# Settling without the high and low split, 64-column w1 products, zeros and biases earlier, experts' inputs five pairs ahead

## The chip, the cores and the metric

One core of one Trainium2 chip. The time is the device time of one execution in microseconds (us), the median of several runs.

## What is computed

Two layers over 8192 tokens (16 sequences of 512) of 256 channels. Layer 0 adds to x, from its layer norm, a small gated network on four heads and a mixture of experts; layer 1 adds an attention and a product with a ternary matrix.

```python
xn = _layernorm(x, axis=-1)
x = x + _L0_attn_ref(xn, ...) + _L0_ffn_ref(xn, ...)
xn = _layernorm(x, axis=-1)
x = x + _L1_attn_ref(xn, ...) + _L1_ffn_ref(xn, ...)

# _L0_ffn_ref, 16 experts, the best two of each token
xe = jnp.einsum('bsd,eod->bseo', u, Wr) + br
routed = jnp.einsum('bse,bseo->bso', g_topk, xe)
shared = (jnp.einsum('bsd,eod->bso', u, Ws) + jnp.sum(bs, axis=0)) / N_s
return u + routed + shared

# _L1_ffn_ref
out = jnp.einsum('bsd,od->bso', input, w_ternary * alpha) + bias
```

The gated network needs only the query part of `_L0_attn_ref` in this kernel: q is normalised, goes through w0 and w2 (`tanh` makes the sigmoid), and the hidden vector goes through w1.

## The kernel before

`two_layers` runs four stages one after the other. Each is a block: all five queues (SP, POOL, ACT, DVE, PE) end it together before the next begins. A unit is U = 2 tiles of 128 tokens; there are NU = 32 units. Every engine runs a fixed, written-out list of steps, so the order on each engine is the order of the code, and semaphores do the rest. An SP or POOL queue that waits holds back all transfers behind the wait.

**1. Sorting stage, `route`.** Steps v from -6 to 34; a step works on units v to v+4 at different places of the pipeline. PE: w0 and w2 products in two halves (L609, 64-row tiles), counts of the chosen experts (L621 to L662), transposes (L633, L654), the query and score product (L644), and `psB`, which takes the shared expert (L677) and w1 (L680). ACT evaluates tanh (L348), squares with a sum (L372), copies and normalised rows (L391). DVE multiplies the hidden vector (L439, L442), scales the queries (L536, L545) and chooses the experts (L454 to L489). POOL takes roots and powers and scatters each normalised row to its two experts' regions in `rows_dram` (L313). w1 is kept as 128 columns per head of which 64 are zero, so that both heads of a pair add into all 128 partitions of one bank. In the last steps SP reads, expert by expert, the end of each region into a register (`value_load`) and writes 128 rows of zeros there (L267, 16 transfers), writes two small tables (L260), and stores the parts of the last units (L250). After its last step DVE makes the low halves of the experts' weights (L593, 16 instructions of 128x512).

**2. Experts, `experts`.** 72 pairs of jobs; a job is 128 rows for one expert. SP loads a pair's rows three pairs ahead (`xs`, XS = 8 slots, L753) and stores the pair's result (L762) after waiting for DVE; PE transposes pair n+1 (L816) and then multiplies pair n with 12 products (L834 to L836: high by high, high by low, low by high); ACT takes the high part of the transposed rows (L782), DVE the low part (L790) and adds the expert's bias (L801). The biases of all experts (128 x 4096 numbers) are loaded by SP behind the first six loads (L757). The registers with table entries are loaded eight at a time.

**3. Settling, `settle`.** Per unit: SP loads the part and x (L894, L896) three units ahead, POOL gathers the two expert results of each of the two tiles with four indirect transfers (L939), PE transposes the part (L1041), DVE adds x, the two weighted results, takes mean and variance, adds the bias of the last product (`x1b`, L1012), makes six small factors (L1016 to L1025); POOL takes the root (L948, L950); ACT normalises (L959); PE transposes (L1052); ACT takes the high part (L965), DVE the low part (L975), PE multiplies both with the ternary matrix (L1059, L1060), DVE adds up `base` (L983). SP stores high part, low part and base (L912, L916, L918). SP also loads the first weights of the last stage here.

**4. Attention, `phase_b`.** 256 heads, one per step, 16 steps per sequence. SP loads the high and low parts of the next sequence in step 12 (L1207, L1208). Before the first product ACT and DVE split the first weights (L1323, L1415).

What sets the order in the experts' loads:

```python
for j in range(3 * U):
    load(j)
sp.dma_start(bias_bc[:], io["br"]...partition_broadcast(P)).then_inc(br_in, 16)
for n in range(PAIRS):
    for t in range(U):
        load((n + 3) * U + t)
    need(sp, y_dve, U, n, U)
    sp.dma_start(out_dram[n], ys[:, n % 4]).then_inc(y_out[n % 4], 16)
```

Of the kernel before, what the change touches and what calls it, by code (L numbers as in the profile page):

```python
# [21 lines left out]
F32 = mybir.dt.float32  # L22
# [5 lines left out]
P = 128  # L28
D = 256
# [55 lines left out]
class Kept:  # L85


    def __init__(self, nc, ctx, tiles, jobs):
# [9 lines left out]
        self.wtern = sb("wtern", [P, KD, D], F32R)  # L98
        self.alpha_bc = sb("alpha_bc", [P, 1])
        self.table = sb("table", [1, 2 * 2 * P], mybir.dt.uint32)  # L100

# [7 lines left out]
def route(nc, io, rows, part, region, jobs, kept, raw, wr_hi, raw_in):  # L109
# [5 lines left out]
    with ExitStack() as ctx:  # L115
# [6 lines left out]
        def bank(name, n=1):  # L122
# [3 lines left out]
        w1 = sb("w1", [P, FH, P])  # L126
# [4 lines left out]
        raw_s = sb("raw_s", [P, KD, NS, D])  # L131
        raw_t = sb("raw_t", [P, KD, D])
# [3 lines left out]
        tern = sb("tern", [P, 2, KD, D])  # L136
# [23 lines left out]
        junk = sb("junk", [P, 2, U, D])  # L160
        z2 = sb("z2", [P, 2, U, D])
# [3 lines left out]
        qn = sb("qn", [P, 2, U, D])  # L165
        qt = sb("qt", [P, 2, FH // 2, U, P])
        th = sb("th", [P, 8, 2, U * P])
        acc = sb("acc", [P, 2, U, D])
# [28 lines left out]
         rt_dve, rt_act, c_pe, tb_dve, tb_in, ends_in) = map(sem, (  # L197
             "const_in", "const_pool", "const_dve", "w1_act", "wr_act", "wr_dve", "tern_dve", "tern_pe", "ln_dve", "ln_pool",
             "ln_act", "t_pe", "t_act", "r_pe", "r_act", "r_dve", "z_pool", "zs_dve", "zq_dve", "q_pe", "q_act",
             "g_pe", "g_act", "g_dve", "b_pe", "b_act", "rt_dve", "rt_act", "c_pe", "tb_dve", "tb_in",  # L200
# [3 lines left out]
        POOL_CONST = 4 + 3 + 1 + 2 + 3 + 4  # L204
# [15 lines left out]
        def _(sp):  # L220
# [25 lines left out]
            for v in steps:  # L246
                u = v - 2
                if 0 <= u < NU:
                    need(sp, b_act, 1, u, 1)
                    sp.dma_start(part[u], acc[:, u % 2]).then_inc(stored[u % 2], 16)  # L250
# [6 lines left out]
                if v == NU:  # L257
                    sp.wait_ge(tb_dve, 13)
                    for k in range(2):
                        sp.dma_start(kept.table[0:1, k * 2 * P:(k + 1) * 2 * P].rearrange("a (p h) -> a p h", p=P),  # L260
                                     jobs_u[:, k]).then_inc(tb_in, 16)
# [10 lines left out]
            sp.wait_ge(tb_in, 32)  # L272
            for r in range(2):
                sp.wait_ge(stored[r], 16 * (NU // 2))

        @block.gpsimd
        def _(g):
# [10 lines left out]
            const(g.memset(w1[:], 0.0))  # L288
# [1421 lines left out]
```

## Time and profile before

| | us |
|---|---|
| median of 3 runs | 3041.45 |
| lowest, highest | 3036.73, 3049.71 |
| the profiled execution: its time | 3047.77 |
| the profiled execution: its span | 3046.0 |
| busy PE, DVE, ACT, POOL | 2774.1, 2111.6, 1841.7, 1995.8 |
| mean granted TensorE clock | 0.952 of full speed |

The profiled execution's own time is 1.8 us more than its span, which goes from its first to its last instruction. Busy times are sums over four stages of very different limits. The queues of the transfers and semaphore instructions are not counted as busy. In a timeline each row gives the start, the duration, engine, line and operation, what it writes and reads, and in brackets how long the engine had been idle before it and what released it. A product of plain float32 numbers has two records on PE, one of the fp32r kind has one.

### The profile page before, as it was taken

Reading aid. Unit: us, or ns where it says so; the run is one execution under the profiler, and the core shown is the slowest. Engines: PE = TensorE matmul, PEld = TensorE weight load, DVE = VectorE, ACT = ScalarE, POOL = GpSimd, SP = SyncE. Lnnn points to the kernel's source line nnn. Section 1 sums busy time; section 2 is a strip of 40 time slices with the busy share of each in tenths; the row PEclk is TensorE's granted clock in tenths of the full one; section 3 lists DMA queues with packets and bytes.
Section 4 is the critical chain, followed back from the end, with each engine's and each line's share of the span. In section 5 each row is a group of like instructions: output and inputs, shape, how many; then the busy total and the mean of one; then the engine's idle time right before and its main releaser. Section 6 shows DMA issues by size and latency. Waiting matters only on the chain.

```text
span 3046.0 us, 46091 instructions
## 1 busy us (share of the span) xinstructions
PE 2774.1 (91%) x13314; PEld 2043.3 (67%) x13314; DVE 2111.6 (69%) x3578; ACT 1841.7 (60%) x2651; POOL 1995.8 (66%) x1246
## 2 busy tenths in 40 slices
PE   6999678555499999999999999999999999999997
PEld 4555377444366777777777777777777777777775
DVE  6878555688766666767676766667666666767663
ACT  4555222122267777767676777777777777777774
POOL 4666500477257777777777777777777777777775
PEclk9999899666699999999999999999999999999998
DMA  4432367798512232222222222232322222231321
GB/s 135 133 124 91 134 206 216 219 266 254 176 42 67 49 74 54 68 69 52 69 54 68 58 64 63 58 76 45 74 53 71 58 62 75 43 79 43 79 48 48
DMA packets 271646, 282.95 MB, mean 93 GB/s; under 512 B 97344, under 2 KB 214336, under 8 KB 271424
## 3 DMA queue, kind: packets, MB, share of 16 engines
q1 hardware_dynamic: 259264, 248.25, 30.8%
q0 software_dynamic: 12288, 33.57, 3.6%
q8 instruction: 44, 0.72, 0.1%
q14 instruction: 50, 0.41, 0.0%
HBM read 131.76 MB, written 82.31 MB: 70 GB/s over the span
## 4 chain that ended last, share of the span: by engine, by line
PE 70%; POOL 1%; DVE 1%; ACT 1%; DMA 0%; issue 0%; SPq 0%; POOLq 0%; ACTq 0%; DVEq 0%
PE psV_b L1581 8%; PE psV_b L1576 8%; PE psV_b L1577 8%; PE psS_b L1564 8%; PE psS_b L1563 7%; PE psN_b L1549 7%; PE psY_b L1504 4%; PE psX_b L1504 4%; PE psY_b L1505 4%; PE psY_b L1506 4%; PE psX_b L1505 4%; PE psX_b L1506 4%; POOL pp_lo_b L1294 1%; PE psN_b L1633 0%; DVE vals_lo_b L1472 0%
## 5 line engine op out<-in xcount | busy, mean ns | idle before, releaser
L1294 POOL TENSOR_TENSOR pp_lo_b<-pf_b,pp_hi_b 128x1024 fp32r<-128x1024 f32 x512 | 1229.7, 2402 | 604.3 <-ACT pp_hi_b L1336 517.9
L1440 DVE TENSOR_REDUCE negmax_b<-psN_b 128x2 fp32r<-128x1024 f32 x512 | 626.9, 1224 | 379.1 <-PE psN_b L1549 371.8
L1331 ACT ACTIVATE pf_b<-psS_b 128x1024 f32<-128x1024 f32 x512 | 526.1, 1028 | 238.4 <-PE psS_b L1564 235.2
L1563 PE MATMUL psS_b<-qA_b,kA_b 128*128 128x512 f32 x1024 | 405.8, 396 | 6.8 <-DVE qB_b L1455 5.0
L1564 PE MATMUL psS_b<-qB_b,kB_b 68*128 68x512 f32 x1024 | 406.6, 397 | 0.0
L1577 PE MATMUL psV_b<-pp_hi_b,vals_lo_b 128*64 128x512 f32 x1024 | 403.6, 394 | 0.0
L1576 PE MATMUL psV_b<-pp_hi_b,vals_hi_b 128*65 128x512 f32 x1024 | 402.0, 393 | 1.7 <-DVE vals_lo_b L1472 0.2
L1355 ACT ACTIVATE kA_b<-psX_b 64x512 fp32r<-64x512 f32 x256 | 152.0, 594 | 289.4 <-PE psX_b L1506 284.6
L1549 PE MATMUL psN_b<-kA_b,qA_b 128*128 128x512 f32 x1024 | 322.6, 396 | 4.7 <-DVE negmax_b L1440 4.2
L1581 PE MATMUL psV_b<-pp_lo_b,vals_hi_b 128*65 128x512 f32 x1024 | 320.2, 394 | 5.1 <-POOL pp_lo_b L1294 5.1
L1336 ACT ACTIVATE pp_hi_b<-pf_b 128x1024 fp32r<-128x1024 f32 x256 | 271.5, 1061 | 8.1
L1429 DVE SCALAR_TENSOR_TENSOR kB_b<-psX_b,kA_b 64x512 fp32r<-64x512 f32 x256 | 176.2, 688 | 140.1 <-ACT kA_b L1355 136.0
L1563 PEld LDWEIGHTS psS_b<-qA_b,kA_b 128*128 128x128 f32 x1024 | 193.6, 189 | 65.9 <-DVE qB_b L1455 7.2
L1450 DVE CAST pp_hi_b<-pf_b 128x1024 fp32r<-128x1024 f32 x256 | 233.0, 910 | 5.3 <-ACT pf_b L1331 5.3
L1549 PEld LDWEIGHTS psN_b<-kA_b,qA_b 128*128 128x128 f32 x1024 | 192.2, 190 | 55.1 <-DVE negmax_b L1440 7.2
L1308 POOL TENSOR_TENSOR otf_b<-outs,inverse_b 128x512 f32<-128x512 f32 x128 | 211.1, 1649 | 20.8 <-DMA inverse_b<-inverse_dram 18.6
L1504 PE MATMUL psX_b<-xT_hi,wqkv_hi_b 128*128 128x512 f32 x512 | 210.8, 412 | 13.9 <-DVE wqkv_lo_b L1415 8.4
L1564 PEld LDWEIGHTS psS_b<-qB_b,kB_b 68*128 68x128 f32 x1024 | 193.6, 189 | 40.5
L1581 PEld LDWEIGHTS psV_b<-pp_lo_b,vals_hi_b 128*65 128x65 f32 x1024 | 137.7, 135 | 105.7 <-POOL pp_lo_b L1294 9.7
L1505 PE MATMUL psX_b<-xT_lo,wqkv_hi_b 128*128 128x512 f32 x512 | 203.7, 398 | 0.0
L1506 PE MATMUL psX_b<-xT_hi,wqkv_lo_b 128*128 128x512 f32 x512 | 203.4, 397 | 0.0
L1429 DVE SCALAR_TENSOR_TENSOR qA_b<-psX_b,qA_b 64x512 fp32r<-64x512 f32 x256 | 176.5, 690 | 38.2 <-ACT qA_b L1355 34.2
(209 smaller groups left out, 5623.6 us busy)
## 6 DMA issues: line engine op xcount, KB each, us to landing
kA_b<-kA_b SPq DMA_DIRECT2D x128, 256.0 KB, 3.2
qB_b<-qA_b SPq DMA_DIRECT2D x128, 256.0 KB, 2.9
inverse_b<-inverse_dram SPq DMA_DIRECT2D x256, 128.0 KB, 3.1
xs_e<-rows_dram SPq DMA_DIRECT2D x144, 128.0 KB, 2.6
results_dram<-ys_e SPq DMA_DIRECT2D x72, 256.0 KB, 2.4
x_a<-x_dram SPq DMA_DIRECT2D x16, 512.0 KB, 4.7
part_dram<-acc_a SPq DMA_DIRECT2D x32, 256.0 KB
acc_s<-part_dram SPq DMA_DIRECT2D x32, 256.0 KB
```

The lines of the kernel that those rows point to most:

```text
L1294: pool.tensor_tensor(pp[1][:, c], pf[:, c], pp[0][:, c].bitcast(F32), ALU.subtract).then_inc(pl_pool, 1)
L1331: a.activation(pf[:, c], psS[:], ACT.Exp).then_inc(exp_act, 1)
L1440: v.tensor_reduce(negmax[:, n.slot(2), 2 * c:2 * c + 2], psN[:], AX.X, ALU.max, negate=True).then_inc(mx_dve, 1)
L1504: pe.matmul(out, lh, rh, start=start, stop=False)
L1505: pe.matmul(out, lh, rl, start=False, stop=False)
L1506: return pe.matmul(out, ll, rh, start=False, stop=stop)
L1549: mm = pe.matmul(psN[:, t], qA[:, s, i * P:(i + 1) * P], kA[:, s], start=True, stop=True)
L1563: pe.matmul(psS[:, t], kA[:, s, keys], qA[:, s], start=True, stop=False)
L1564: mm = pe.matmul(psS[:, t], kB[:, s, keys], qB[:, s], start=False, stop=True)
L1576: pe.matmul(psV[0:DH + 1, g.slot(2)], values(0, h, i), pp[0][:, c, t], start=(i == 0), stop=False)
L1577: pe.matmul(psV[0:DH, g.slot(2)], values(1, h, i), pp[0][:, c, t], start=False, stop=False)
L1581: mm = pe.matmul(psV[0:DH + 1, g.slot(2)], values(0, h, i), pp[1][:, c, t], start=False, stop=(i == TB - 1))
```

## The change

- `route`: w1 is kept as 64 columns per head; the two heads of a pair write partitions 0 to 63 and 64 to 127 of the bank. The bias load is moved from the experts to step 17 of this stage. The 16 zero writes and both tables are issued by SP in step NU-1, ahead of the part of that step, with eight ends loaded into registers at once. DVE makes the low halves of four weight pieces after the tables, of four more before the last hidden product, and of eight at the end. `raw_s`, `raw_t`, `tern` lie in the bias tile, `junk`, `z2`, `qn`, `acc` in the tiles that the settling loads into.
- `experts`: twelve slots and loads five pairs ahead; no bias load and no wait for it; near the end SP issues the first three units' loads of the settling.
- `settle`: the part and x are joined on PE (x by identity, then the part against the identity, both into one bank); no DVE addition of x, no `x1b`, no low part; the ternary product is plain float32 of the unsplit rows; one transposed copy is stored (two stores per unit fewer); the factors of unit u follow the sums of unit u+1 and the end of unit u-1; POOL gathers two units at first and a third after the root.
- `phase_b`: one load of the unsplit rows per sequence (step 11) into two slots of `ot`; ACT makes the high part (step 12), DVE the low part in two pieces (steps 12 and 13); the ternary bias is added by DVE in steps 3 to 6. For the first sequence both parts are made ahead of the first product.

```diff
@@ route
-                if NU - 1 <= v <= NU:
-                    if v == NU - 1:
-                        sp.wait_ge(tb_dve, 1)
-                    for e in range((v - NU + 1) * NE // 2, (v - NU + 2) * NE // 2):
-                        at = sp.value_load(ends_u[0:1, e:e + 1], min_val=0, max_val=NE * region - P)
-                        sp.dma_start(rows[bass.ds(at, P), :], zeros[:]).then_inc(ends_in, 16)
+                if v == 17:
+                    sp.wait_ge(tern_dve, 11)
+                    sp.dma_start(bias_bc[:], io["br"].rearrange("e n -> (e n)").partition_broadcast(P)).then_inc(br_in, 16)
+                if v == NU - 1:
+                    sp.wait_ge(tb_dve, 1)
+                    for h in range(2):
+                        at = nc.values_load_multi_w_load_instructions(
+                            ends_u[0:1, h * 8:(h + 1) * 8], engines=[mybir.EngineType.SP], min_val=0, max_val=NE * region - P,
...
+                        for e in range(8):
+                            sp.dma_start(rows[bass.ds(at[e], P), :], zeros[:]).then_inc(ends_in, 16)
...
                 if s == NU - 1:
                     make_tables()
+                    weights_low(0, 4)
...
+                if s == NU - 1:
+                    weights_low(4, 8)
                 if 0 <= s < NU:
                     hidden_product(s, 1)
...
+            weights_low(8, 16)
...
-                        mm = pe.matmul(psB[:, 0], w1[:, 2 * m + j], th[:, first:first + 3:2, j], start=False, stop=(j == 1))
+                        mm = pe.matmul(psB[j * FD:(j + 1) * FD, 0], w1[:, 2 * m + j], th[:, first:first + 3:2, j], start=False, stop=True,
+                                       skip_group_check=True)
@@ experts
-        XS = 8
+        XS = 12
...
-            for j in range(3 * U):
+            for j in range(5 * U):
                 load(j)
-            sp.dma_start(bias_bc[:], io["br"].rearrange("e n -> (e n)").partition_broadcast(P)).then_inc(br_in, 16)
             for n in range(PAIRS):
                 for t in range(U):
-                    load((n + 3) * U + t)
+                    load((n + 5) * U + t)
                 need(sp, y_dve, U, n, U)
                 sp.dma_start(out_dram[n], ys[:, n % 4]).then_inc(y_out[n % 4], 16)
+                if n >= PAIRS - 5 and n < PAIRS - 2:
+                    ahead.load(sp, n - PAIRS + 5)
@@ settle
-            for u in range(3):
-                gather(u)
+            gather(0)
+            gather(1)
             for u in range(NU):
-                need(g, s_dve, SD, u, 9)
-                need(g, s_dve, SD, u - 2, SD)
+                need(g, s_dve, SD, u, SD)
+                need(g, f_dve, FC, u - 2, FC)
...
-                gather(u + 3)
+                if u < 2:
+                    gather(u + 2)
+                if u >= 1:
+                    gather(u + 3)
...
+            for u in range(NU + 2):
+                if u < NU:
+                    gathered(u)
+                if 0 <= u - 1 < NU:
+                    factors(u - 1)
+                finish(u - 2)
...
                     for t in range(U):
+                        pe.matmul(psA[:, u % 2, t * D:(t + 1) * D], kept.ident[:], x[:, u % 4, t], start=True, stop=False,
+                                  skip_group_check=True)
                         for m in range(KD):
                             at = (t * KD + m) * P
-                            mm = pe.transpose(psA[:, u % 2, at:at + P], acc[:, u % 4, m, t * P:(t + 1) * P], kept.ident[:])
+                            mm = pe.matmul(psA[:, u % 2, at:at + P], acc[:, u % 4, m, t * P:(t + 1) * P], kept.ident[:], start=False,
+                                           stop=True, skip_group_check=True)
...
-                        pe.matmul(out, xrt[0][:, u % 2, t, k], kept.wtern[:, k], start=(k == 0), stop=False)
-                        mm = pe.matmul(out, xrt[1][:, u % 2, t, k], kept.wtern[:, k], start=False, stop=(k == KD - 1))
+                        mm = pe.matmul(out, xrt[:, u % 2, t, k], kept.wtern[:, k], start=(k == 0), stop=(k == KD - 1))
@@ phase_b
-            for c in SPLITS[-4]:
+            split_low(0)
+            for k in range(KD):
+                rows_low(Step(None, 1, 0), xT[1][:], k)
+            for c in SPLITS[-4][1:]:
                 split_low(c)
```

## Rows read from the trace of the kernel before

**Rows 1.** Stages: us, busy PE, PEld, DVE, ACT, POOL, clock, DMA share, GB/s.

```profile
60.00:360.00 300.00, 274.02 (x1276) 162.37 (x1276) 235.94 (x698) 155.32 (x361) 197.41 (x203) 0.99 0.35 116
...
380.00:558.00 178.00, 142.29 (x1118) 133.30 (x1116) 102.17 (x214) 41.33 (x69) 7.74 (x14) 0.96 0.69 209
...
580.00:740.00 160.00, 85.35 (x352) 68.99 (x352) 142.31 (x421) 37.16 (x66) 114.61 (x133) 0.63 0.88 258
...
1000.00:1500.00 500.00, 499.73 (x2365) 370.20 (x2364) 348.00 (x441) 356.48 (x470) 368.76 (x179) 1.00 0.27 64
```

**Rows 2.** Timeline of the sorting stage, the round from one count to the next.

```profile
197.18 0.30 PE L621 MATMUL psC_a<-mask_a,before_a 128*128 128x64 f32 x1 [0.57 <-DVE mask_a L480]
...
198.14 2.00 PE L644 MATMUL psR_a<-wq_a,xt_a 128*128 128x272 f32 x8
...
201.05 0.69 DVE L545 TENSOR_TENSOR qw_a<-psR_a,qw_bc_a 128x512 f32<-128x512 f32 x1 [0.53 <-ACT junk_a L372]
...
204.29 1.88 PE L680 MATMUL psB_a<-th_a,w_a 128*128 128x512 f32 x4
...
207.66 0.58 ACT L348 ACTIVATE th_a<-psG_a 128x512 f32<-128x512 f32 x1
...
216.88 0.30 PE L621 MATMUL psC_a<-mask_a,before_a 128*128 128x64 f32 x1 [0.77 <-DVE mask_a L480]
```

**Rows 3.** Timeline of the sorting stage's end and the first row of the experts.

```profile
338.47 0.17 DVE L500 TENSOR_TENSOR ends_u_a<-psC_a,ebase_a 128x16 uint32<-128x16 f32 x1
...
348.87 9.71 DVE L593 TENSOR_TENSOR wr_raw<-wr_raw,wr_hi 128x512 fp32r<-128x512 f32 x16
...
355.62 0.69 ACT L365 ACTIVATE acc_a<-psB_a,mean_b_a 128x512 f32<-128x512 f32 x1 [3.85 <-PE psB_a L680]
...
357.19 7.97 SPq L267 DMA_DIRECT2D rows_dram<-zeros_a  x8
365.20 0.43 SPq L250 DMA_DIRECT2D part_dram<-acc_a  x1
367.83 0.29 POOL L768 COPY moved_e<-place_f 128x128 f32<-128x128 f32 x1 [21.52 <-POOLq L115]
```

**Rows 4.** Timeline of the experts; the last row is the loads' time from issue to landing.

```profile
381.03 0.76 DVE L801 TENSOR_TENSOR ys_e<-psY_e,bias_bc_e 128x256 f32<-128x256 f32 x2 [4.87 <-DMA bias_bc_e<-br_dram]
...
383.86 0.42 SPq L762 DMA_DIRECT2D results_dram<-ys_e  x1
...
385.37 0.43 SPq L762 DMA_DIRECT2D results_dram<-ys_e  x1
...
387.93 0.51 PE L816 MATMUL psT_e<-ident_r,xs_e 128*128 128x128 f32 x4 [0.39 <-DMA xs_e<-rows_dram]
...
549.43 0.46 PE L816 MATMUL psT_e<-ident_r,xs_e 128*128 128x128 f32 x4
...
551.23 0.46 PE L816 MATMUL psT_e<-ident_r,xs_e 128*128 128x128 f32 x4
...
DMA to landing us min/median/max: 2.0/2.6/7.4
```

**Rows 5.** Timeline of the settling; last, one of DVE's groups (busy us, mean ns).

```profile
558.36 0.36 SPq L894 DMA_DIRECT2D acc_s<-part_dram  x1
...
624.07 0.20 POOL L948 TENSOR_TENSOR vs_s<-mv_s,eps_s 128x4 f32<-128x4 f32 x1 [0.73 <-DVE stats_s L1006]
...
631.41 0.20 POOL L948 TENSOR_TENSOR vs_s<-mv_s,eps_s 128x4 f32<-128x4 f32 x1 [1.06 <-DVE mv_s L1010]
...
L1012 DVE TENSOR_TENSOR x1b_s<-x_s,fbias_bc_s 128x512 f32<-128x512 f32 x22 | 15.0, 680 | 0.0
```

**Rows 6.** Timeline of the attention: its start, and ACT after step 12.

```profile
810.26 0.91 SPq L1204 DMA_DIRECT2D pf_b<-w_qkv_dram  x2
...
815.25 0.76 PE L1504 MATMUL psX_b<-xT_hi,wqkv_hi_b 128*128 128x512 f32 x1 [8.41 <-DVE wqkv_lo_b L1415]
...
1224.88 1.03 ACT L1331 ACTIVATE pf_b<-psS_b 128x1024 f32<-128x1024 f32 x1 [1.20 <-PE psS_b L1564]
```

More of the change, by code:

```diff
@@ L247, in _ @@
                 u = v - 2
+                if v == 17:
[6 more added lines that the diff above has]
+                            ends_u[0:1, h * 8:(h + 1) * 8], engines=[mybir.EngineType.SP], min_val=0, max_val=NE * region - P,
+                            skip_runtime_bounds_check_because="an end is a region's base and a count of at most N rows", bass_reorder=False)[1]
+                        for e in range(8):
+                            sp.dma_start(rows[bass.ds(at[e], P), :], zeros[:]).then_inc(ends_in, 16)
+                    sp.wait_ge(tb_dve, 13)
+                    for k in range(2):
+                        sp.dma_start(kept.table[0:1, k * 2 * P:(k + 1) * 2 * P].rearrange("a (p h) -> a p h", p=P),
+                                     jobs_u[:, k]).then_inc(tb_in, 16)
                 if 0 <= u < NU:
@@ L519, in make_tables, with weights_low @@
                                        op0=ALU.mult, op1=ALU.add).then_inc(tb_dve, 1)
+            def weights_low(first, end):
+                for c in range(first, end):
+                    at = weights_of_experts(c)
+                    v.wait_ge(wr_act, c + 1)
+                    v.tensor_tensor(raw[at].bitcast(F32R), raw[at], wr_hi[at].bitcast(F32), ALU.subtract).then_inc(wr_dve, 1)
             for s in steps:
@@ L837, in _, with settle @@
                 mm.then_inc(y_pe, 1)
-def settle(nc, io, results, part, xT_hi, xT_lo, base_dram, early, kept):
+def settle(nc, io, results, part, xT_dram, base_dram, early, kept, ahead):
     NU = part.shape[0]
@@ L1243, in step @@
                 done = pair_at(g, -3)
+                if g.const % H == 11 and g.within(0, NH) and batch(g, 1).within(0, B):
+                    after(sp, o_pe, 8, batch(g, -1), 8)
+                    load_x(batch(g, 1))
                 if g.const % 2 == 1:
@@ L1444, in step @@
                     maximum(0)
+                t = g.const % H - 3
+                if 0 <= t < TB and batch(g, -1).within(0, B):
+                    b = batch(g, -1)
+                    if b.reg is None and b.const == 0:
+                        v.wait_ge(fb_in, 16)
+                    after(v, o_dve, 8, b, t + 1)
+                    v.tensor_tensor(acc[:, t], acc[:, t], fbias_bc[:], ALU.add).then_inc(fb_dve, 1)
+                if g.const % H == 13 and g.within(0, NH) and batch(g, 1).within(0, B):
+                    rows_low(batch(g, 1), raw_x, 1)
                 if n.within(0, NH):
@@ L1526, in kq @@
                 if which == 0:
[L1527 removed]
+                    after(pe, xl_dve, KD, b, KD)
                     after(pe, kq_dve, 4, p + -1, 4)
@@ L1657, in two_layers @@
             kept = Kept(nc, first, N // P, jobs)
+            ahead = Ahead(nc, first, io, part)
             with ExitStack() as hold:
```

249 lines of the change are left out of this document (117 added, 132 removed).

## The prediction

> **What bounds the kernel now.** I read the busy times by stage first, then each stage's timeline at the place where its slowest engine waits. The stages follow one another with all queues joined in between, so each has its own bound and the gains add up. In the attention PE is busy 499.73 of 500 us [rows 1]: only fewer products could shorten it, and the change takes none away there. In the settling PE is busy 85 of 160 us at a mean clock of 0.63, DVE 142, POOL 115, and the transfers hold 88% of their engines [rows 1]. One unit takes 631.41 - 624.07 = 7.34 us, and POOL idles only 1.06 us of it, waiting for DVE [rows 5]: DVE is the bound, POOL is next. In the experts no engine but PE is over 60% busy (142 of 178), and the transfers have 69% [rows 1]. A pair takes (551.23 - 387.93) / 66 = 2.47 us on average, but the last, whose inputs have long landed, 1.80 us [rows 4]. What is missing is the rows' arrival. The sorting stage looks bound by PE, 274 of 300 us [rows 1]. It isn't quite, and that decides what the 64-column products are worth.
>
> **Sorting stage, w1.** One unit has two w1 products of 512 columns, four records, 1.88 us [rows 2]. With 64 columns each they write different halves of the partitions, and if the halves run side by side they take half, 0.94 us less. Now follow what carries one round (two units) to the next: the count product at 197.18 waits for DVE's mask; behind it on PE comes the score product at 198.14; ACT squares its result and DVE, idle for it, begins `qw` at 201.05; DVE then works without a pause up to the scores' maximum; ACT's exp and tanh follow, the tanh at 207.66, straight behind exp and a cast, so that it is not PE that it waits for; DVE continues to the next mask, and the next count product starts at 216.88, after PE had idled 0.77 us for it [rows 2]. That ring takes 19.7 us here (19.5 is the usual distance), and w1, at 204.29, is not in it. PE runs beside the ring and arrives 0.57 to 0.77 us early each time. A shorter w1 makes PE idle longer. I put its gain at 1 us in all, part of the rounding; its bounds are 0 and 0.94 x 32 less the cost of a switch, about 26 us.
>
> What speaks against it is a rule in the Trainium skill, TensorEngine Tiling (Array Packing), Tiling Modes: going from one tiling to another drains the array. The same page gives two 64-column tiles up to twice the speed. By the first a unit pays two more drains, by the second it saves the 0.94 us; neither reaches the ring, so the sum is the same by both.
>
> **Sorting stage, end.** DVE makes 16 low halves in 9.71 us from 348.87 to 358.58; SP is later still: its second eight zero writes run from 357.19 to 365.16, the last part goes out at 365.20, and the next stage begins at 367.83, 2.2 us after that issue [rows 3]. One zero write with its register costs 7.97 / 8 = 1.00 us With eight ends loaded at once and all 16 writes in step NU-1, begun at 338.64 when the ends are there [rows 3], they and the tables are out by about 350, under work that PE and DVE have yet to do. What is late next: the last part. It was ready at 355.62 + 0.69 = 356.3, released by the last w1 product [rows 3]; two w1 products lie on that tail and each is 0.94 us shorter, so it goes out at about 354.8 (0.4 us given back for DVE's four low halves before the hidden product), and the stage ends 2.6 us later, 357.4. DVE then has eight low halves at the end, 4.9 us, done by 354. Gain 367.8 - 357.4 = 10.4 us. If the w1 pair does not run side by side it is 9; if SP's writes still end last, at worst 16 x 1.0 from 338.7 plus tables and parts, 359, it is 8.5.
>
> The bias load, 2 MB, now lies in step 17, where the transfers are 35% busy [rows 1] and x is loaded three groups ahead. POOL makes one memset less. I cost both at nothing; without that cover the load would be the same 5 us that it takes from the experts now.
>
> **Experts.** The bias load goes from the front, where DVE waited 4.87 us for it [rows 4] and the first rows queued behind it. From the first transposes to the sixth pair took some 15 us; with PE at half clock for the first ones I expect 11.5: 3.4 us. For the other 66 pairs: a load goes out after DVE has finished pair n-1, about 1.0 us into pair n; issue and two loads take 1.2, landing 2.6 at the median [rows 4]; it is wanted two pairs after the start of pair n. (1.0 + 1.2 + 2.6) / 2 = 2.4 us, which is the measured 2.47. So the distance sets the pace. With two pairs more the same delay is spread over four: 1.2 us, no longer a bound. Next are three floors close to each other: PE 1.80; SP, which needs 385.37 - 383.86 = 1.51 us for a store and two loads where it never waits [rows 4], some 1.8 with registers and its odd long issues; and the transfers, 0.69 x 2.47 = 1.70 us at 100%. I take 1.95, near the floors (the row of the last pair is what remains without waiting) with 0.15 for their coupling; ends 1.80 and 2.47. 66 x (2.47 - 1.95) = 34.3. The six loads for the settling add SP time that hides under 1.95, but 1.5 MB runs beside the last stores: 1 us back. Sum 37 us.
>
> **Settling.** DVE loses three instructions of 128x512 at 0.68 [rows 5] and, because the factors come one unit later, the wait for POOL's root: 7.34 - 2.0 - 0.3 = 5.0 us. POOL keeps its four gathers and two small operations: 7.34 - 1.06 = 6.28 us of the unit it is busy, and with a wake-up of 0.17 a unit takes 6.45. Two 512-byte-run stores fewer take load off the transfers (0.88 x 7.34 = 6.5 us per unit before, and one of seven parts by bytes goes: 5.5). PE gets more: a plain product of 272 columns takes 2.00 / 4 = 0.50 us at full clock [rows 2], so 256 columns take 0.47. Per unit there are two for x, four of 128 columns (0.24) for the part, four transposes (about 0.24), four ternary products of 256: 0.94 + 0.96 + 0.96 + 1.88 = 4.7 us at full clock, plus ACT's copy of 0.6 between: 5.3. That fits into 6.45; at half clock it is 10.0. PE was at 53% busy and half clock most of the time [rows 1]; a PE that never rests is granted the full clock in rows 1, so I take POOL's 6.45. Ends: 6.3 and, with a clock that alternates, 7.1 (4.7 / 0.75 + 0.6 = 6.9). The stage took 810.26 - 558.36 = 251.9 us [rows 5, 6], 32 x 7.34 = 234.9 and 17.0 of start and tail. The start loses a wait for loads that are now there, the tail gains slower products; I leave it at 17. New: 223.4. Gain 28.5 us.
>
> **Attention.** ACT's high part of the first sequence (128x1024, about 1.0 by the row of that size) and DVE's two low parts (2 x 0.68 by [rows 5]) come before the first product, which DVE's first split releases at 815.25 [rows 6]; ACT's is beside that split, DVE's are behind it: 1.5 us later. In the loop ACT gets 1.0 us once in 16 steps, just where it idled 1.20 us [rows 6]; DVE gets six instructions per sequence, 0.4 to 0.7 us each, into gaps of about 0.9, and is 70% busy [rows 1]. Nothing; without that cover 3 us per sequence, 45 in all, which I bound at 5 because PE is behind none of them. Cost 1.5 us.
>
> **Sum.** -10.4 - 37 - 28.5 + 1.5 = -74.4 us against the profiled execution's 3047.77, which is 6.3 above the median of the runs. Against the median: 3041.45 - 74.4 = 2967 us. One measurement of this kernel tells 0.5%, 15 us, from no change.
>
> **Rivals.**
> *PE does bound the sorting stage.* For it: 91% busy, and waits of 0.2 to 0.8 us only. Against: it is PE that waits in the ring, at both ends [rows 2]. Then 26 us more are won: 2941. Chance 10%.
> *The rows stay late.* If SP's long issues or the transfers' queue, not the distance, make the landing late (7.4 us at most [rows 4]), a pair still takes 2.3: 66 x 0.17 + 3.4 = 14 instead of 37: 2990. Against it is the fit of the 2.4 us. Chance 15%.
> *PE at a changing clock in the settling,* 7.0 us per unit: 32 x 0.55 = 18 us less gain, 2985. Chance 9%.
> *PE at half clock is the settling's bound,* and the kernel gets slower. Place: the plain ternary and x products, behind which every unit's `base` waits. Price: 10.0 us per unit with ACT's copy, less what overlaps, say 9.5 to 10.0: 32 x (9.8 - 7.34) = +79 against -46 of the rest: 3041 + 33 = 3074. It decides from 7.34 + 46 / 32 = 8.8 us per unit. For it speaks the 0.63 of rows 1; against it, that half clock was seen there only with PE idle half the time. Chance 3%.
> By the Trainium skill, TensorE: Matmul & The Clock Gate, Part 4, transposes do not count as PE work for the clock as other products do. The change makes products of the part's transposes, so by that rule this rival is less likely still; no row here separates the two kinds.
> *The change doesn't do what it says:* gains in the middle are paid back by a wait that I don't see (SP blocked by step 17's wait, or rows of x behind the bias): within 15 us of before. Chance 3%.
> The forecast has 60%.
>
> **Numbers.** Faster by over 0.5%: 60 + 10 + 15 + 9 = 94, less 1 for two bad cases together, 93%. Slower by over 0.5%: 2%, most of the half-clock case. The rest 5%. The range goes from the first rival with the floors of the experts, 2935, to the late rows with some loss in the settling, 3005.
>
> **What would show it.** Sorting stage: the same 19.5 us per two units, w1's four records in about 1 us, longer waits of PE for the mask, and the experts' first row 10 us earlier. Experts: no wait for the bias, hardly any of the transposes for `xs`, pairs 1.9 to 2.0 us apart. Settling: POOL without the 1.06 us wait, units 6.45 apart, a clock above 0.63. Attention: PE as full as before, steps of 8.5 us. The forecast is wrong if rounds of the sorting stage become shorter, if pairs stay above 2.2 us, or if PE is what settling units wait for.

## The result and the profile after

The changed kernel takes 2967.2 us at the median of 4 runs (2964.8 to 2968.5), the kernel before 3043.7 in as many (3036.7 to 3049.7): a ratio of 0.975, 95% interval 0.973 to 0.977. The profiled executions are 3047.77 and 2968.46 us, 79.3 apart, a little more than the medians (76.5). All of it is in the first quarter of the span. Windows of the kernel after (us, busy PE, PEld, DVE, ACT, POOL, clock, DMA share, GB/s), to be laid beside [rows 1]:

```profile
60.00:360.00 300.00, 259.51 (x1274) 148.81 (x1273) 235.74 (x696) 152.91 (x359) 196.09 (x205) 0.96 0.38 127
362.00:510.00 148.00, 135.56 (x1152) 132.76 (x1152) 104.10 (x216) 43.10 (x72) 15.71 (x28) 0.96 0.87 267
560.00:700.00 140.00, 104.71 (x533) 86.82 (x531) 97.93 (x356) 37.15 (x66) 113.41 (x133) 0.94 0.83 255
1000.00:1500.00 500.00, 499.66 (x2341) 369.34 (x2340) 364.04 (x466) 362.12 (x477) 370.31 (x176) 1.00 0.25 56
```

In the experts PE went from 80% busy to 92, and the transfers from 0.69 to 0.87. In the settling the clock went from 0.63 to 0.94, and POOL, 72% busy before, is at 81% (with the 0.3 us between two gathers, which are not counted, it is full). The attention is as it was.

The stages follow one another, so the first row of the next one bounds each: POOL's first row for the experts and the settling, SP's first for the attention. All lengths below are read so, from the profiled execution of each kernel; the experiments are explained in the next section.

| kernel | sorting | experts | settling | attention |
|---|---|---|---|---|
| before | 367.8 | 190.5 | 251.9 | 2235.7 |
| after | 359.1 | 151.3 | 219.7 | 2236.6 |
| before, narrow w1 (b_w1) | 366.4 | 187.2 | 251.2 | 2231.8 |
| wide w1 (a_w1wide) | 360.0 | 153.0 | 219.9 | 2233.7 |
| zeros late (a_zeros_late) | 364.9 | 157.6 | 218.9 | 2237.0 |
| biases late (a_bias_late) | 354.8 | 159.0 | 220.9 | 2238.8 |
| 3 pairs ahead (a_ahead3) | 356.5 | 191.1 | 220.5 | 2233.9 |
| 4 pairs ahead (a_ahead4) | 357.3 | 164.8 | 219.5 | 2239.2 |
| 6 pairs ahead (a_ahead6) | 355.1 | 150.4 | 219.5 | 2237.5 |
| 3 gathers (a_gather3) | 358.3 | 152.0 | 186.1 | 2238.1 |
| 3 additions on DVE (a_dve_load) | 356.2 | 151.8 | 239.5 | 2234.4 |
| roots on ACT (a_sqrt_act) | 359.2 | 151.2 | 252.3 | 2238.0 |
| the same, paced (a_sqrt_paced) | 359.9 | 152.8 | 244.6 | 2240.5 |
| the same, with an addition (a_sqrt_tick) | 359.0 | 151.7 | 193.1 | 2236.4 |

Stages that a kernel has in common with others differ by up to 5 us in the sorting and 7 in the attention; a difference below that is read from the medians, or not at all.

**End of the sorting stage**, timeline of the kernel after (start, duration, engine, line; to be laid beside [rows 3]). SP's zero writes now run under the last rounds, the last part (the third of the group at 348.60, released by ACT's row at 355.94) is what ends last, and the experts begin at 359.14 instead of 367.83:

```profile
338.03 9.26 SPq L273 DMA_DIRECT2D rows_dram<-zeros_a  x16
347.34 1.22 SPq L276 DMA_DIRECT2D table<-jobs_u_a  x2
348.60 8.37 SPq L280 DMA_DIRECT2D part_dram<-x_s  x3
...
348.99 4.90 DVE L540 TENSOR_TENSOR wr_raw<-wr_raw,wr_hi 128x512 fp32r<-128x512 f32 x8
...
354.81 1.08 PE L701 MATMUL psB_a<-th_a,w_a 128*64 128x512 f32 x4
355.94 0.69 ACT L380 ACTIVATE x_s<-psB_a,mean_b_a 128x512 f32<-128x512 f32 x1 [3.16 <-PE psB_a L701]
359.14 0.29 POOL L790 COPY moved_e<-place_f 128x128 f32<-128x128 f32 x1 [13.63 <-POOLq L132]
```

**Experts**, SP's timeline of the kernel after (to be laid beside [rows 4]): one store per pair. The 64 pairs from 380.90 to 502.01 take 1.89 us each; where nothing disturbs them the stores are 1.80 apart, PE's own work on a pair:

```profile
380.90 1.01 SPq L782 DMA_DIRECT2D results_dram<-ys_e  x1
...
401.86 0.38 SPq L782 DMA_DIRECT2D results_dram<-ys_e  x1
403.67 0.38 SPq L782 DMA_DIRECT2D results_dram<-ys_e  x1
405.47 0.80 SPq L782 DMA_DIRECT2D results_dram<-ys_e  x1
...
502.01 0.36 SPq L782 DMA_DIRECT2D results_dram<-ys_e  x1
```

**Settling**, POOL's timeline of the kernel after (to be laid beside [rows 5]). Between two units POOL waits for no engine any more: 6.30 us, four gathers of 0.95 with 0.3 between them and 1.3 for the roots:

```profile
640.56 0.21 POOL L962 TENSOR_TENSOR vs_s<-mv_s,eps_s 128x4 f32<-128x4 f32 x1
640.85 1.03 POOL L964 TENSOR_TENSOR root_s<-vs_s,power_s 128x4 f32<-128x4 f32 x1
642.08 1.02 POOL L953 DMA_INDIRECT y_s<-results_dram,place  x1 [0.19 <-issue]
643.40 0.95 POOL L953 DMA_INDIRECT y_s<-results_dram,place  x1 [0.30 <-issue]
644.65 0.95 POOL L953 DMA_INDIRECT y_s<-results_dram,place  x1 [0.30 <-issue]
645.90 0.94 POOL L953 DMA_INDIRECT y_s<-results_dram,place  x1 [0.30 <-issue]
646.86 0.22 POOL L962 TENSOR_TENSOR vs_s<-mv_s,eps_s 128x4 f32<-128x4 f32 x1
```

**Attention**, its start in the kernel after (to be laid beside [rows 6]): the first product comes 6.2 us after SP's first row instead of 5.0, and DVE's low part of the rows is what it waits for:

```profile
730.12 0.34 SPq L1238 DMA_DIRECT2D fbias_bc_b<-fbias_dram  x1
...
736.36 0.76 PE L1545 MATMUL psX_b<-xT_hi,wqkv_hi_b 128*128 128x512 f32 x1 [9.69 <-DVE xT_lo L1447]
```

### The profile page after: what moved, and what is told of

It is laid out like the page before. It is cut to its first block, busy times and chain, and to the rows that moved or that the text cites. A ratio compares the mean times of both kernels' runs of the same rounds, so it can differ in the third digit from the quotient of the medians.

```text
span 2966.7 us, 46545 instructions
## 1 busy us (share of the span) xinstructions
PE 2779.6 (94%) x13570; PEld 2053.6 (69%) x13570; DVE 2107.0 (71%) x3578; ACT 1854.8 (63%) x2664; POOL 2012.4 (68%) x1245
## 4 chain that ended last, share of the span: by engine, by line
PE 71%; POOL 1%; DVE 1%; ACT 1%; DMA 1%; issue 0%; SPq 0%; POOLq 0%; ACTq 0%; DVEq 0%
PE psV_b L1622 8%; PE psV_b L1617 8%; PE psV_b L1618 8%; PE psS_b L1605 8%; PE psS_b L1604 8%; PE psN_b L1590 8%; PE psY_b L1545 4%; PE psX_b L1545 4%; PE psY_b L1546 4%; PE psY_b L1547 4%; PE psX_b L1546 4%; PE psX_b L1547 4%; POOL pp_lo_b L1309 1%; PE psN_b L1674 1%; DVE vals_lo_b L1508 0%
## 5 line engine op out<-in xcount | busy, mean ns | idle before, releaser
L1374 ACT ACTIVATE kA_b<-psX_b 64x512 fp32r<-64x512 f32 x256 | 152.0, 594 | 289.4 <-PE psX_b L1547 284.5
L1486 DVE CAST pp_hi_b<-pf_b 128x1024 fp32r<-128x1024 f32 x256 | 241.7, 944 | 5.3 <-ACT pf_b L1350 5.3
L1491 DVE TENSOR_TENSOR qB_b<-psN_b,own_tile_b 4x512 fp32r<-4x512 f32 x256 | 173.3, 677 | 42.4 <-PE psN_b L1674 40.4
```

## The experiments

Ratios are to the kernel before in the same session; the change's own is 0.975, and 0.001 is 3 us.

**The w1 products.** Two runs: the kernel before with the narrow products alone, and the changed kernel without them.

```diff
-        w1 = sb("w1", [P, FH, P])
+        w1 = sb("w1", [P, FH, FD])
-   mm = pe.matmul(psB[:, 0], w1[:, 2 * m + j], th[...], start=False, stop=(j == 1))
+   mm = pe.matmul(psB[j * FD:(j + 1) * FD, 0], w1[:, 2 * m + j], th[...], start=False, stop=True, skip_group_check=True)
```

> The kernel before with the 64-column w1 products alone. My theory (PE is not in the ring of a round): rounds stay near 19.5 us, the four w1 records take 1.08 us instead of 1.88, PE waits longer for the mask, the whole is within 3 us of before (ratio 0.999 to 1.001), and the experts' first row comes at 366 to 368 us. Rival (PE bounds the sorting stage): 26 us faster, rounds of 18 us, ratio 0.991. Second rival (a longer idle makes the granted clock fall, as in two rounds of the changed kernel that took 21.6 and 21.4 us): one to three rounds of about 21.5 us, and up to 5 us slower.

> The changed kernel with w1 padded to 128 columns again. My theory: rounds of 19.5 us, w1 1.88 us again, the whole 0 to 2 us slower (two w1 products on the stage's tail). Rival (PE bounds the sorting stage): 26 us slower. Second rival (the shorter w1 costs clock): the two rounds of 21.5 us become 19.5, the stage ends 2 to 4 us earlier and the whole is 1 to 3 us faster.

Measured: b_w1 3041.7 us, ratio 0.9987 (0.9978 to 0.9997); a_w1wide 2971.7 us, 0.9758 (0.9744 to 0.9771). By the ratios the products are worth 4 us in the first (1 to 7 by its interval) and 3 in the second, whose interval overlaps the change's own; both are a little more than was expected. The 26 us of the PE-bound case are excluded from both sides. PE's timeline, wide (first two rows) and narrow (the rows of the kernel after):

```profile
176.82 0.30 PE L646 MATMUL psC_a<-mask_a,before_a 128*128 128x64 f32 x1 [0.65 <-DVE mask_a L499]
173.22 1.88 PE L705 MATMUL psB_a<-th_a,w_a 128*128 128x512 f32 x4
```

```profile
153.21 1.08 PE L701 MATMUL psB_a<-th_a,w_a 128*64 128x512 f32 x4
...
156.66 0.30 PE L642 MATMUL psC_a<-mask_a,before_a 128*128 128x64 f32 x1 [1.12 <-DVE mask_a L495]
```

What PE saves, it mostly waits: 0.65 us for the mask become 1.12, and where the first gated product of a unit waits for DVE's `th`, 0.24 become 0.95 (at 150.06 in a_w1wide, 149.84 in the kernel after). ACT's exp of the routing scores marks the rounds. In the run a_ahead3, whose sorting stage is the changed one, its 15 starts span 50.81 to 319.12, 268.3 us; in a_w1wide 50.16 to 320.73, 270.6: in some rounds PE does count, by 0.4 to 0.7 us (19.0 instead of 19.4), 2.2 us in all. Against that, six of the twelve profiles with narrow products have one or two rounds that are about 1.7 us longer than in the others, as the expectation's last case had it; the two with wide ones have none. In the kernel after it is two. Windows over such a stretch (the clock is the last number but two), and the score products in it, which take 2.00 us at the full clock:

```profile
172.00:176.00 4.00, 3.32 (x15) 1.15 (x13) 3.73 (x12) 2.20 (x6) 1.91 (x3) 1.00 0.24 89
176.00:180.00 4.00, 3.41 (x13) 2.92 (x14) 2.82 (x8) 2.56 (x5) 3.20 (x3) 0.66 0.10 35
```

```profile
177.83 3.41 PE L665 MATMUL psR_a<-wq_a,xt_a 128*128 128x272 f32 x8
```

In each of these rounds the granted clock falls to its lower level (1.2 GHz) for some 4 us; here it does so under the score product, which is in the ring. The product takes 1.4 us more, the round 1.7. So a kernel with the shorter products gains 2.2 us in its rounds and sometimes loses as much. That the longer idle time of PE makes the clock fall is not shown: in a_ahead3 the waits ahead of the same place are the same to 0.02 us (1.29, 0.18 and 1.12 against 1.30, 0.16 and 1.11) and the clock stays full, and two profiles with wide products are too few to say that it does not happen there.

**The zeros.** The zero writes with a register load each, and the tables, behind the last parts again:

```diff
-                    for h in range(2):
-                        at = nc.values_load_multi_w_load_instructions(ends_u[0:1, h * 8:(h + 1) * 8], ...)[1]
-                        for e in range(8):
-                            sp.dma_start(rows[bass.ds(at[e], P), :], zeros[:]).then_inc(ends_in, 16)
...
+                if NU - 1 <= v <= NU:
+                    for e in range((v - NU + 1) * NE // 2, (v - NU + 2) * NE // 2):
+                        at = sp.value_load(ends_u[0:1, e:e + 1], min_val=0, max_val=NE * region - P)
+                        sp.dma_start(rows[bass.ds(at, P), :], zeros[:]).then_inc(ends_in, 16)
```

> The changed kernel with the zero writes, their single register loads and the tables at their old place, behind the last parts. My theory: SP ends last again, the experts' first row at 367 to 369 us instead of 359.1, the whole 8 to 10 us slower: 2976. Rival (the stage's end is set by PE and the last part, SP only fills that time): within 2 us of the changed kernel.

Measured: 2975.3 us, ratio 0.9765 (0.975 to 0.978), 5 to 8 us slower, a little less than expected. From the last exp to the experts' first row it is 45.2 us (319.74 to 364.91), against 37.0 in the kernel after (322.10 to 359.14) and 46.3 in the one before: nearly all that is gained at the stage's end is SP's queue. (The experts were 6 us longer in this one profile, its slowest execution, with six waits of PE for rows instead of one; that was not followed up.)

**The biases.** Their load behind the experts' first ten:

```diff
-                if v == 17:
-                    sp.wait_ge(tern_dve, 11)
-                    sp.dma_start(bias_bc[:], io["br"]...).then_inc(br_in, 16)
...
             for j in range(5 * U):
                 load(j)
+            sp.dma_start(bias_bc[:], io["br"]...).then_inc(bias_in, 16)
```

> The changed kernel with the experts' biases (2 MB) loaded behind the experts' first loads again, now ten of them, instead of in step 17 of the sorting stage. My theory: DVE waits 3 to 5 us for it, the loads behind it are late once, the whole is 3 to 6 us slower: 2971. Rival (hidden by rows that are loaded five pairs ahead): under 1 us. Rival on the other side (the load in step 17 delays x in the sorting stage): the sorting stage 2 us shorter, the whole less than 2 us slower.

Measured: 2974.4 us, ratio 0.9762 (0.9747 to 0.9777), 4 us slower by the ratios and 7 by the medians. The experts are 7.7 us longer; the sorting stage's rounds are the same with and without the load (268.3 us between the first and the last exp here too), so that in step 17 it costs nothing. DVE's row at the front (timeline of the experts in a_bias_late):

```profile
362.38 0.42 SPq L774 DMA_DIRECT2D bias_bc<-br_dram  x1
...
371.73 0.76 DVE L820 TENSOR_TENSOR ys_e<-psY_e,bias_bc 128x256 f32<-128x256 f32 x2 [8.85 <-DMA bias_bc<-br_dram]
```

**How far ahead.** Three kernels, 3, 4 and 6 pairs instead of 5, with 8, 10 and 14 buffers; the first one's edit:

```diff
-        XS = 12
+        XS = 8
-            for j in range(5 * U):
+            for j in range(3 * U):
-                    load((n + 5) * U + t)
+                    load((n + 3) * U + t)
```

> The changed kernel with eight row buffers and loads three pairs ahead, as before the change. My theory (distance sets the pace, (1.0 + 1.2 + landing) / 2): with the landing of 2.6 us of before 2.4 us per pair, the experts 31 to 36 us longer, the whole about 3001. Rival (the bias load at the front was what kept the rows late): pairs near 1.9 us, the whole within 5 us of the changed kernel.

> The changed kernel with ten buffers and loads four pairs ahead. By the same formula (1.0 + 1.2 + 2.6) / 3 = 1.6 us, below PE's 1.80, and with a landing of 3.5 us 1.9: pairs of 1.90 to 1.95 us, the whole 0 to 4 us slower than the changed kernel. Rival (the landing grows with the load on the transfers, so that five pairs are needed): 2.1 us per pair, the whole 14 us slower.

> The changed kernel with fourteen buffers and loads six pairs ahead. Three pairs ahead took 2.45 us per pair, four 2.10, five 1.89; PE's own work is 1.80 and the transfers' 1.70. If lateness still costs 0.09 us: 1.82 to 1.86 us, the whole 2 to 5 us faster. Rival (the transfers at 0.9 of their time keep the last 0.09): the same within 1.5 us.

Measured: 3 ahead 3006.3 us, 0.987 (0.985 to 0.989); 4 ahead 2981.8, 0.9778 (0.9762 to 0.9794); 6 ahead 2965.2, 0.9745 (0.973 to 0.976), no different from 5. Three ahead gives back all 40 us of the experts' stage, with the bias load still out of the way: the distance was the cause. The stage is then even 0.6 us longer than in the kernel before, which has the bias load at its front: from the first transposes to the sixth pair's it is 2.0 us shorter without that load (12.9 against 14.9), and the 66 pairs behind them take 2.7 us more together. At this distance, moving the load shows no gain. Four ahead went against my formula, which had 1.6 to 1.9 us per pair, and came out as the rival had it, 2.1; it is 13.5 us longer than five, so 1.89 + 13.5 / 72 = 2.08. The waits of a_ahead4 between 375 and 500 us (engine, line, waited for: us in total, times, longest), and the loads' time from issue to landing with 3, 4 and 5 ahead:

```profile
PE psT_e L836 <- DMA xs_e<-rows_dram: 7.3, 7, 2.0
```

```profile
DMA to landing us min/median/max: 1.9/2.6/4.9
```

```profile
DMA to landing us min/median/max: 2.0/3.3/5.2
```

```profile
DMA to landing us min/median/max: 1.9/3.5/5.2
```

Two things are not in the formula. The landing grows with the transfers' share: between 385 and 495 us that is 0.69, 0.82 and 0.91 with 3, 4 and 5 ahead (which of the two drives the other, or whether it is the number of loads under way, these runs do not separate). And the late ones count, not the median: four ahead leaves 3 pairs, 5.4 us, for the 1.0 and 1.2 before a load is out and a landing of 3.3 at the median, but of 5.2 for the latest, which is 2.0 us too much, the longest wait above. Such a wait is not made up, since PE has nothing to spare at 1.80. The waits for rows are 7.3 us of the 13.5; another 5.3 stand in the same list without a releaser, and what they are is open. At five the waits for rows are all but gone, and the sixth pair ahead finds nothing.

**What sets a settling unit.** One gather of four left out; and three additions given back to DVE:

```diff
-                        for k in range(TOP):
+                        for k in range(TOP - t):
...
-  in0=y[:, u % 4, t, 1], scalar=kept.share[1][:, n:n + 1]
+  in0=y[:, u % 4, t, 1 - t], scalar=kept.share[1][:, n:n + 1]
```

> The changed kernel with three gathers in a settling unit instead of four: for the second tile the first expert's row stands in for the second's, so that one expert's share is left out there. My theory (POOL sets the unit, 4 x 1.25 + 1.31 = 6.31 us): 5.1 to 5.4 us per unit, the whole 29 to 38 us faster: about 2934. Rival (PE at a changing clock sets it): 6.2 us, within 4 us. Rival (the transfers): 0.8 x 6.3 = 5.0 us of work less one sixth, so between 5.4 and 6.0 us per unit, 10 to 29 us faster.

```diff
                 need(v, s_dve, SD, u, 4)
+                for i in range(3):
+                    v.tensor_tensor(spare[:, i], x1[:, u % 3], x1[:, u % 3], ALU.add)
```

> The changed kernel with three additions of 128x512 of no use put back on DVE in each settling unit, as much as the change took off it (2.0 us). My theory (POOL sets the unit at 6.31 us, DVE has 2.2 us to spare): 6.4 to 6.7 us per unit, the whole 3 to 12 us slower. Rival (DVE's three instructions were the gain): 7.2 to 7.4 us per unit, the whole 29 to 34 us slower.

Measured: a_gather3 2934.0 us, ratio 0.962 (0.9601 to 0.964). The stage is 33.6 us shorter, 1.05 per unit, for one gather of 1.25; the clock is full and the transfers are at 0.95 of their time (windows):

```profile
580.00:660.00 80.00, 67.15 (x378) 57.01 (x376) 68.84 (x248) 26.42 (x47) 66.16 (x79) 1.00 0.95 280
```

a_dve_load 2984.9 us, 0.9808 (0.9793 to 0.9823): 0.62 us per unit longer, between my theory (0.1 to 0.4) and the rival (0.9 to 1.1). POOL's timeline in it shows why: it still waits for nobody, but its two small operations are longer than without DVE's additions.

```profile
614.42 0.48 POOL L963 TENSOR_TENSOR vs_s<-mv_s,eps_s 128x4 f32<-128x4 f32 x1
614.98 1.37 POOL L965 TENSOR_TENSOR root_s<-vs_s,power_s 128x4 f32<-128x4 f32 x1
616.54 1.01 POOL L954 DMA_INDIRECT y_s<-results_dram,place  x1 [0.19 <-DVE mv_s L1019]
...
621.36 0.27 POOL L963 TENSOR_TENSOR vs_s<-mv_s,eps_s 128x4 f32<-128x4 f32 x1
```

The two small operations take 0.48 + 1.37 instead of 0.21 + 1.03 (0.32 and 1.37 at the median of the 32 units, against 0.21 and 1.04). POOL remains the bound, at 6.9 us here. The Trainium skill, GPSIMD Engine Reference, Key points, says that POOL shares its SBUF interfaces with DVE and that DVE instructions with two SBUF inputs contend for them; these additions are such, and the rows agree. No run here has additions with one such input, so that it is the second input that matters is not shown.

**Taking the roots off POOL.** If POOL is the bound, 1.3 us of roots per unit should be worth 30 us. They go to ACT (two square roots and, on DVE, one more reciprocal):

```diff
-                g.tensor_tensor(vs[...], mv[...], eps[:], ALU.add)
-                g.tensor_tensor(root[...], vs[...], power[:], ALU.pow)
+                for i in range(2):
+                    a.activation(root[:, u % 2, i], mv[:, u % 2, :, 1], ACT.Sqrt, bias=eps[:, i, 0:1])
...
+                v.reciprocal(rin[:, u % 2], root[:, u % 2, 0])
```

> The changed kernel with the two roots of a settling unit made on ACT (two square roots of 128x2 and one more reciprocal on DVE) instead of on POOL (1.31 us per unit). My theory (POOL sets the unit): POOL is left with 4 x 1.25 = 5.0 us, units of 5.1 to 5.5 us, the whole 26 to 38 us faster: about 2935. Rival (the chain over DVE, ACT and PE sets it): units of 6.0 us or more, under 10 us faster. Rival (the transfers, which hold 0.87 of 6.3 us in the first units): 5.5 us in those, 5.1 in the rest.

Measured: 3002.1 us, ratio 0.9846 (0.9829 to 0.9863): 30 us slower by the ratios and 35 by the medians, outside all that was expected. Every second or third unit follows the last by 4.7 to 4.9 us, and behind it everything stands still: the next takes 9 to 10. Timeline of a_sqrt_act, POOL, DVE and ACT:

```profile
531.41 0.95 POOL L953 DMA_INDIRECT y_s<-results_dram,place  x1 [0.30 <-DVE mv_s L1022]
...
531.80 0.17 DVE L1027 RECIPROCAL rin_s<-root_s 128x2 f32<-128x2 f32 x1 [0.52 <-issue]
532.57 0.16 DVE L1029 TENSOR_TENSOR fac_s<-rin_s,root_s 128x2 f32<-128x2 f32 x1 [0.60 <-DVE rin_s L1027]
533.97 0.17 DVE L1031 TENSOR_SCALAR fac_s<-fac_s 128x2 f32<-128x2 f32 x1 [1.24 <-DVE fac_s L1029]
...
545.14 0.94 POOL L953 DMA_INDIRECT y_s<-results_dram,place  x1 [0.30 <-issue]
548.72 0.88 DVE L999 SCALAR_TENSOR_TENSOR base_s<-psF_s,fac_s,x_s 128x256 f32<-128x256 f32 x2 [9.63 <-remote]
551.01 0.60 ACT L987 ACTIVATE xrt_s<-psT_s 128x512 f32<-128x512 f32 x1 [10.28 <-remote]
```

POOL issues gathers from 511.27 to 546.08 without a break, 28 in a row, 0.3 us between them and no other instruction; the last twelve begin at 531.41. DVE's little instructions, which wait only for each other and otherwise follow at 0.2 us, now start 0.8 to 2.1 us apart; `base` (L999), whose products had ended at 534.9, starts at 548.72; ACT idles 10.28 us, though the transposes it waits for (L1073) had ended at 541.5. Both go on only after the last gather. SP's queue is silent too, from 534 to 551.63, but that proves nothing: its next transfer is the store of what ACT has not made yet.

Is it that gathers run too far ahead, or that they run without a break? Two more kernels: first the wait of the changed kernel put back, so that the gathers of unit u+3 follow the statistics of unit u; then one addition of 128x2 ahead of each four (the first added line is a_sqrt_paced, all three are a_sqrt_tick).

```diff
+                need(g, s_dve, SD, u, SD)
+                g.tensor_tensor(tick[:, u % 2], eps[:, 0], power[:, 0], ALU.add).then_inc(tick_pool, 1)
+                g.wait_ge(tick_pool, u + 1)
```

> The kernel with the roots on ACT, whose units took 7.9 us where POOL ran up to twelve gathers ahead without a pause and stores on SP's queue landed up to 10 us late, with one wait put back: POOL's gathers of unit u+3 go out only when DVE has finished the statistics of unit u, as in the changed kernel. Theory A (the gathers that run ahead fill the queue before what is wanted next): units of 5.1 to 5.5 us, the whole about 2935. Theory B (POOL's unbroken sequence of gathers is the harm, however far ahead): stalls of several us again, the whole above 2975. Theory C (the longer chain over ACT and DVE is slow by itself): even units of 6.3 us or more without long stalls, the whole 2967 or more.

> The roots on ACT and the wait put back, as in the run before that stalled, and now one small addition on POOL (128x2, about 0.2 us) ahead of each unit's four gathers, which POOL waits for. If it is the unbroken sequence of gathers that keeps the other engines' waits from ending, and any other instruction of POOL between them breaks it: no stalls, units of 5.3 to 5.6 us, the whole about 2940, faster than the changed kernel. If a break must be as long as the 1.3 us that the roots took on POOL, or the sequence is not the cause: stalls of several us again, units of 7 us and more, the whole above 2985.

Measured: paced 2998.1 us, 0.9846 (0.9831 to 0.9861), with waits of up to 10.3 us again, most of them behind runs of eight gathers. So it is not only how far ahead they run. (The stores that landed up to 10 us late, of which the expectation speaks, are not in the profile of a_sqrt_act: it gives no landing for them, and the first long wait of ACT is for no store.) With the addition 2942.0 us, 0.9667 (0.9641 to 0.9693): no such wait, units of 5.2 us. POOL's timeline of a_sqrt_tick:

```profile
602.39 0.20 POOL L963 TENSOR_TENSOR tick_s<-eps_s,power_s 128x2 f32<-128x2 f32 x1
602.86 0.96 POOL L955 DMA_INDIRECT y_s<-results_dram,place  x1 [0.27 <-POOL tick_s L963]
604.13 0.95 POOL L955 DMA_INDIRECT y_s<-results_dram,place  x1 [0.30 <-issue]
605.38 0.95 POOL L955 DMA_INDIRECT y_s<-results_dram,place  x1 [0.30 <-issue]
606.63 0.94 POOL L955 DMA_INDIRECT y_s<-results_dram,place  x1 [0.30 <-issue]
607.59 0.21 POOL L963 TENSOR_TENSOR tick_s<-eps_s,power_s 128x2 f32<-128x2 f32 x1
```

An instruction of 0.2 us with a wait for its end, 0.5 us per unit, shortens the stage by 51 us (244.6 to 193.1). It is not the bare number of gathers in a row either: in a_sqrt_tick eight go out together behind one addition, from 527.85 to 537.57, and DVE's little instructions still follow at 0.2 to 0.4 us. This kernel is 25 us faster than the changed one, and its interval doesn't touch that one's.

## Why the prediction was right, point by point

The direction, the stages and the mechanisms were right, and so was the time, within 0.2 us. That closeness is luck: the sum said -74.4 against the profiled execution, and that difference was -79.3; against the medians it was -76.5, and the median of before came out 2.2 us higher, with one more run, than the one that the forecast started from. Stage by stage the gain measured less the gain forecast is -1.7, +2.2, +3.7 and +0.6 us. So the sum was 2 to 5 us short, and the rest of the agreement is in the runs.

- **Sorting stage, w1: "1 us in all".** Right in kind: 3 to 4 us by the two runs, nothing in the rounds of the kernel after itself. PE is not in the ring in most rounds; in some it is by half a us, which I had not seen (2.2 us), and in the kernel after two rounds at the lower clock take that back. As for the rule of the Trainium skill that was weighed (TensorEngine Tiling (Array Packing), Tiling Modes), that a change of tiling drains the array: the four records take 1.08 us where two perfect halves would take 0.94, so the halves do run side by side. From the first of them to the product behind them it is 1.01 us in one unit of a round and 1.18 in the other, where the wide ones take 1.81 and half of that is 0.91: whatever the switches cost is 0.1 to 0.3 us per unit.
- **Sorting stage, end: 10.4, bounds 8.5 to 10.4.** Mis-sized a little: from the last exp on it is 46.3 - 37.0 = 9.2 us, of which 8.1 are the zeros and tables (45.17 - 37.04, by a_zeros_late) and about 1 is the rest. The stage as a whole gained 8.7. The last part goes out at 356.6, not 354.8: counted from the last exp, ACT's last row comes 0.2 us earlier than before, not 1.5. The traces show why. The shorter w1 products do give what was priced, since in a_w1wide that row comes 36.1 us behind the last exp and in the kernel after 33.8. But the shared expert's products of the two units before the last took 1.96 and 2.52 us before and 3.76 and 3.78 after, and from 346 to 350 us the granted clock was 0.76 before and 0.50 after. In a_w1wide they take 3.18 and 3.68, so the narrow products are not the reason; what else is, stays open. The step that is off is the tail worked out at an unchanged clock. The second of the two in the kernel after (2.52 before, from 346.80):

```profile
346.93 3.78 PE L698 MATMUL psB_a<-xt_a,wshare_a 128*128 128x512 f32 x4
```

- **The bias load at nothing in step 17.** Right, by the rounds of a_bias_late.
- **Experts: 37, measured 39.2.** The pace was taken as 1.95 and is 1.89, PE's own 1.80 being the floor, as said: 38.5 us instead of 34.3. From the first transposes to those of the sixth pair it is 11.4 us (11.5 forecast, 14.9 before). The two ends give back 2.9 us, not 1: the first transposes come 0.5 us later behind the stage's start, and from the last ones to its end it is 2.4 us longer. The front's gain belongs to the bias load and the distance together: putting the load back costs 4 to 7 us with five pairs ahead, and leaving it out gains nothing with three. The step that does not hold is the formula, "the same delay is spread over four: 1.2 us, no longer a bound". It gives 2.4 us for three pairs ahead, where it was fitted (2.47 before, 2.51 in a_ahead3), but 1.6 for four, where 2.08 were measured. The answer for five stood because there the margin is large enough.
- **Settling: 28.5, measured 32.2.** POOL is the bound, its 1.06 us of waiting is gone, and the unit is 6.3 instead of 6.45: the wake-up of 0.17 us that I added is not there, since POOL is never behind anyone. PE is busy 4.7 us per unit, as worked out; DVE 4.4 instead of 5.0. Start and tail take 18 us, not 17. What the sum treated as one, DVE's lighter load and the later factors, a_dve_load takes apart: with 2.0 us of work back on DVE POOL still waits for nobody, so its wait went with the order of the steps, and the stage keeps 12.4 of its 32.2 us. The other 19.8 hang on DVE's load, mostly by way of POOL's longer small operations, which is not the way that the sum had it. (The three additions are not the same instructions as those that the change removed.)
- **Attention: 1.5 lost, measured 0.9.** The first product comes 1.2 us later, for the reason given. The rest is below what profiles of the same stage differ by.
- **Rivals.** PE as the bound of the sorting stage and the late rows were excluded by runs (b_w1, a_w1wide; a_ahead3). The changing clock in the settling did not come: 0.94, and POOL covers it. PE at half clock did not either; the price of that case was not measured. A wait that pays the gains back did not come.

## What to carry to other kernels

Find the ring that carries one round to the next before pricing a shorter instruction: what is not in it returns as idle time. For loads ahead, take the late landings at the transfers' future load, not today's median, and try one step more and one less. Where an engine is the bound by a chain of small things, look at what the others do beside it (two-input additions on DVE stretched POOL), and be ready for gathers on POOL to behave differently once the other instructions between them are gone.

## What the hardware showed that was not expected

- Where POOL has nothing but gathers and waits in its stream, DVE, ACT and PE stand still for up to 10 us behind runs of eight and more of them: waits on one's own engine come through at about the spacing of the gathers (1.4 us against 1.25), and finished work of others is taken up as much as 9.5 us late. With the roots or one 0.2 us addition ahead of each unit's four, the kernel after and a_sqrt_tick show none of it. How many gathers do no harm behind such an instruction (eight did none, once in each of these two), whether it is the instruction or the wait for its end that helps, and what is held up, is open; no run here separates them.
- The three DVE additions of 128x512, which have two SBUF inputs, stretch POOL's power from 1.04 to 1.37 us and its addition from 0.21 to 0.32 (medians over 32), which is most of the 0.6 us by which a unit grows.
- With 0.8 us less PE work in a unit of a stage in which PE was 91% busy, between 60 and 320 us of the run the granted clock was at its lower level for a few us in six of twelve profiles, and in neither of the two with the work as it was. The product of 2.00 us under it took 3.41. Whether the shorter products are the cause, two profiles can't tell.
